# A graph layer on one core: the first adjacency unit multiplied piece by piece, its layer norm moved to GpSimd

## What is computed

```python
h = jnp.maximum(_layernorm(x, axis=-1), 0.0)          # x: 4096 x 128
# for each of two branches (features h, and features x2), adj: 4096 x 4096
ax = a @ x
h = ax + (1.0 + eps[0]) * ax
for i in range(3):
    h = jax.nn.relu(h @ W[i].T + b[i])
# then
merged = jnp.concatenate((out1, out2), axis=1)
x = x + merged @ Wm.T + bm
```

## Time and profile before

| | us |
|---|---|
| median of three runs | 408.82 |
| lowest and highest run | 408.42, 409.11 |
| the profiled execution, its whole time | 408.38 |
| its span, first to last instruction | 406.9 |
| PE busy | 402.3 (99%) |
| DVE busy, ACT busy | 219.5, 220.2 (54% each) |
| POOL busy | 30.2 (7%) |

### The profile page before, as it was taken

The page is one execution under the profiler, slowest core; times in us unless marked ns, Lnnn a source line. Parts: engine busy times, 40 slices in busy tenths (PEclk is TensorE's granted clock), DMA queues, the critical chain, the costliest instruction groups (busy, mean ns, idle before and its releaser), DMA issues.

```text
span 406.9 us, 4872 instructions
## 1 busy us (share of the span) xinstructions
PE 402.3 (99%) x1774; PEld 328.7 (81%) x1774; DVE 219.5 (54%) x260; ACT 220.2 (54%) x259; POOL 30.2 (7%) x35
## 2 busy tenths in 40 slices
PE   8999999999999999999999999999999999999996
PEld 3888888888888888888888888888888888888886
DVE  5888887655455334551645517445373444755223
ACT  5876667658474623555434556334565335766034
POOL 1223332100000000000100001000000000000100
PEclk9999999999999999999999999999999999999999
DMA  7998785744645174235584336653175550840100
GB/s 259 423 404 308 304 317 208 254 186 132 232 180 176 58 258 184 106 132 200 149 315 152 114 146 231 233 206 130 77 258 206 206 198 35 270 170 0 52 2 26
DMA packets 14317, 76.21 MB, mean 187 GB/s; under 512 B 1952, under 2 KB 2208, under 8 KB 6368
## 3 DMA queue, kind: packets, MB, share of 16 engines
q1 hardware_dynamic: 12960, 71.97, 47.4%
q0 software_dynamic: 1200, 3.93, 3.0%
q10 hardware_dynamic: 144, 0.13, 0.1%
HBM read 73.93 MB, written 2.10 MB: 187 GB/s over the span
## 4 chain that ended last, share of the span: by engine, by line
PE 99%; DVE 0%; issue 0%; DVEq 0%
PE acc L510 25%; PE acc L506 25%; PE acc L507 25%; PE second_acc L506 3%; PE second_acc L510 3%; PE second_acc L507 3%; PE hidden L507 3%; PE hidden L506 3%; PE hidden L510 3%; PE merged L514 2%; PE merged L507 1%; PE merged L506 1%; PE merged L510 1%; PE acc L534 0%; PE acc L549 0%; PE acc L544 0%
## 5 line engine op out<-in xcount | busy, mean ns | idle before, releaser
L506 PE MATMUL acc<-adj_hi,feat_lo 128*128 128x512 f32 x440 | 171.8, 390 | 0.0
L510 PE MATMUL acc<-adj_lo,feat_hi 128*128 128x512 f32 x440 | 171.7, 390 | 0.0
L507 PE MATMUL acc<-adj_hi,feat_hi 128*128 128x512 f32 x440 | 171.1, 389 | 0.0
L376 DVE TENSOR_TENSOR adj_lo<-adj_raw,adj_hi 128x2048 fp32r<-128x2048 f32 x48 | 108.3, 2288 | 37.9 <-ACT adj_hi L243 36.9
L243 ACT ACTIVATE adj_hi<-adj_raw 128x2048 fp32r<-128x2048 f32 x48 | 90.4, 1926 | 17.6 <-PE acc L510 15.8
L382 DVE TENSOR_TENSOR act_lo<-act_f,act_hi 128x512 fp32r<-128x512 f32 x60 | 41.0, 690 | 105.6 <-ACT act_f L263 105.6
L507 PEld LDWEIGHTS acc<-adj_hi,feat_hi 128*128 128x128 f32 x440 | 82.6, 188 | 17.7
L510 PEld LDWEIGHTS acc<-adj_lo,feat_hi 128*128 128x128 f32 x440 | 82.6, 188 | 17.8
L506 PEld LDWEIGHTS acc<-adj_hi,feat_lo 128*128 128x128 f32 x440 | 82.6, 188 | 17.3
L262 ACT ACTIVATE act_hi<-hidden,bias 128x512 fp32r<-128x512 f32 x45 | 31.0, 688 | 96.2 <-PE hidden L510 96.2
L438 DVE TENSOR_TENSOR adj_lo<-adj_raw,adj_hi 128x2048 fp32r<-128x2048 f32 x14 | 31.7, 2290 | 7.8 <-ACT adj_hi L284 7.8
(11 more groups left out here) (76 smaller groups left out, 238.0 us busy)
## 6 DMA issues: line engine op xcount, KB each, us to landing
adj_raw<-adj_tiles SPq DMA_DIRECT2D x62, 1024.0 KB, 5.1
x_rows<-x_tiles SPq DMA_DIRECT2D x16, 256.0 KB, 6.9
adj_raw<-adj_first SPq DMA_DIRECT2D x8, 256.0 KB, 5.1
x_res<-x_t POOLq DMA_DIRECT2D x8, 256.0 KB, 6.3
out_t<-y_sb POOLq DMA_DIRECT2D x7, 256.0 KB, 2.3
w_raw<-w_t SPq DMA_DIRECT2D x1, 512.0 KB, 5.8
out_t<-y_sb SPq DMA_DIRECT2D x1, 128.0 KB, 1.8
out_t<-y_sb ACTq DMA_DIRECT2D x1, 128.0 KB, 1.8
```

What stands on the lines that cost most here:

```text
L376: nc.vector.tensor_tensor(adj_lo[:, u % RING, :], adj_raw[:, u % RING, :], f32(adj_hi[:, u % RING, :]), ALU.subtract).then_inc(lo_made, 1)
L506: nc.tensor.matmul(out, lhs_lo, rhs_hi, start=start, stop=False)
L507: nc.tensor.matmul(out, lhs_hi, rhs_hi, start=False, stop=False)
L510: return nc.tensor.matmul(out, lhs_hi, rhs_lo, start=False, stop=stop)
```

## The change

- The order on PE is now step 0 for branch 1, step 0 for branch 0, then step 1 for both. Step 0 of branch 1 takes each piece as it comes: high by high, low features by high, and the high by low product of the piece before. The eight products of zeros between the first products are gone; the 15 ahead stay.
- The layer norm of unit 0 leaves ACT. POOL applies scale and shift in four operations of 128x128, in place in `x_rows`; ACT then makes the high part straight from that with a relu; POOL then makes the relu in place for itself (128x512) and subtracts. The other seven units keep their way.
- ACT makes that high part of branch 0 between the high parts of step 0 and those of step 1 (before, after both).
- Step 1 is loaded, and its high and low parts are made, in two halves of 128x1024 instead of four pieces.
- SP waits for the second piece of step 0 before it issues the loads of `x2`, `x` and adjacency of unit 1 and all that follow.

The diff, cut to its core:

```diff
             for s, (u, c) in enumerate(OPENING):
+                if s == len(PIECES):
+                    sp.wait_ge(fine_loaded[1], 16)
                 if c == 0:
                     load_x2(u)
                     load_x(u)
...
+            low_of_x2(0)
+            pool.wait_ge(x_loaded[0], 16)
+            pool.wait_ge(rstd_made, 1)
+            for j in range(JB):
+                last = nc.gpsimd.tensor_scalar(x_rows[:, 0, j, :], x_rows[:, 0, j, :], rstd[:, j:j + 1],
+                                               shift[:, j:j + 1], ALU.mult, ALU.add)
+            last.then_inc(first_norm_made, 1)
+            pool.wait_ge(feat1_hi_made, 1)
+            nc.gpsimd.tensor_scalar(x_rows[:, 0], x_rows[:, 0], 0.0, None, ALU.max).then_inc(first_relu_made, 1)
+            pool.wait_ge(first_relu_made, 1)
+            nc.gpsimd.tensor_tensor(feat_lo[:, 0, 0:JB, :], x_rows[:, 0], f32(feat_hi[:, 0, 0:JB, :]),
+                                    ALU.subtract).then_inc(feat1_lo_made, 1)
...
-            for u in range(U - 2):
+            high_of_x2(0)
+            std_of_x(0)
+            high_of_opening(0)
+            act.wait_ge(first_norm_made, 1)
+            nc.scalar.activation(feat_hi[:, 0, 0:JB, :], x_rows[:, 0], ACT.Relu).then_inc(feat1_hi_made, 1)
+            high_of_opening(1)
+            for u in range(1, U - 2):
...
+                if b == first:
+                    for i in parts:
...
+                        add(feat_hi, adj_hi, i)
+                        if i == 0:
+                            pe.wait_ge(feat2_lo_made, u + 1)
+                        add(feat_lo, adj_hi, i)
+                        if i > 0:
+                            low_ready(i - 1)
+                            add(feat_hi, adj_lo, i - 1)
+                    low_ready(parts[-1])
+                    add(feat_hi, adj_lo, parts[-1])
+                else:
+                    for i in parts:
+                        add(feat_hi, adj_hi, i)
+                    for i in parts:
+                        add(feat_hi, adj_lo, i)
+                    pe.wait_ge(feat1_lo_made, u + 1)
+                    for i in parts:
+                        last = add(feat_lo, adj_hi, i)
+                    signal(u, b, last)
...
+            for at in range(len(PIECES)):
+                for b in BRANCH_ORDER:
+                    pieces_aggregate(at, b)
```

More of the change, by code:

```diff
@@ L120, in gnn_layer_kernel @@
         raw_loaded = [sem(f"raw_loaded{s}") for s in range(RING)]
-        fine_loaded = [sem(f"fine_loaded{s}") for s in range(FINE_LOADS * FINE_SIGNALS)]
+        fine_loaded = [sem(f"fine_loaded{i}") for i in range(sum(len(p) - 1 for p in PIECES))]
         x_loaded = [sem(f"x_loaded{s}") for s in range(X_SLOTS)]
@@ L160, in f32, with piece @@
             return ap.bitcast(F32)
+        def piece(s, i):
+            at = sum(PIECES[s][:i])
+            return range(at, at + PIECES[s][i]), (None if i == len(PIECES[s]) - 1
+                                                  else sum(len(p) - 1 for p in PIECES[:s]) + i)
         def quarter(q):
@@ L193, in _ @@
                     load_x(u)
[L194 to L198, removed]
+                if s < len(PIECES):
+                    source = (adj_first, adj_second)[s]
+                    for i in range(len(PIECES[s])):
+                        js, n = piece(s, i)
+                        cols = slice(js.start * CW, js.stop * CW)
+                        done = raw_loaded[s] if n is None else fine_loaded[n]
+                        sp.dma_start(adj_raw[:, s, cols], source[i]).then_inc(done, 16)
                 else:
@@ L216, in _, with low_of_x2 @@
         def _(pool):
-            for u in range(U):
+            def low_of_x2(u):
                 rows = slice(u * JB, (u + 1) * JB)
@@ L510, in product @@
                 return nc.tensor.matmul(out, lhs_hi, rhs_lo, start=False, stop=stop)
-            def idle_products(n):
-                for _ in range(n):
-                    nc.tensor.matmul(merged[:, :], zeros[:, 0:P], zeros[:, :], start=True, stop=True)
             def columns(u, j):
@@ L521, in opening_bank, with pieces_aggregate @@
                 return (second_acc if c else acc)[b]
[L523 removed]
+            def pieces_aggregate(s, b):
                 u, c = OPENING[s]
                 out = opening_bank(c, b)
[L527 to L551 removed]
@@ new lines, in pieces_aggregate, with add, low_ready @@
+                parts = range(len(PIECES[s]))
+                def add(feat, adj, i):
+                    for j in piece(s, i)[0]:
+                        slot, cols = columns(s, j)
+                        last = nc.tensor.matmul(out[:, :], feat[:, b, u * JB + j, :], adj[:, slot, cols],
+                                                start=(u == 0 and j == 0 and feat is feat_hi and adj is adj_hi), stop=False)
+                    return last
+                def low_ready(i):
+                    n = piece(s, i)[1]
+                    if n is None:
+                        pe.wait_ge(lo_made, s + 1)
+                    else:
+                        pe.wait_ge(fine_lo_made, n + 1)
```

95 lines of the change are left out of this document (40 added, 55 removed).

## The result

The changed kernel takes 410.39 us (median of six runs, 410.37 to 410.85) where the kernel before, in the runs beside it, takes 408.62 (408.29 to 409.11). The ratio is 1.0048, 95% interval 1.0037 to 1.0059: slower, by 1.8 us, where the forecast was 3.25 slower and the range began at 410.0. The profiled execution took 410.85.

What follows compares the result with a forecast made beforehand. PE, busy 99% of the span, was taken as the bound; POOL and DVE taking turns would delay step 2's low part to 23.4 and its product by 3.25 us: 408.82 + 3.25 gives 412.0, range 410.0 to 413.2.

Steps and rivals of the forecast that it cites:

- PE piece by piece: Opening on PE: without the eight zero products, the 12 products of step 0, branch 1 end near 9.9 us.
- The best case: PE's gain in the opening, capped by step 2's low part: product at 19.5 for 20.25, at best 0.75 us won.
- POOL's norm: POOL's four operations alternate with DVE's low parts of step 0 from 7.65; the norm is made at 10.85 us.
- ACT's wait: ACT, done with step 0's copies near 8.85, stands idle some 2 us on POOL ahead of its relu.
- POOL's relu: Unit 0's relu on 128x512, taken as 0.8 us, 11.7 to 12.5; POOL's subtraction then precedes DVE's first half.
- From `var_eps` to the low part of step 2: Unit 1's `var_eps` ends at 19.0; 4.43 us later, at 23.4, step 2's low part ends (19.42 before).
- PE's own stalls: PE's waits for branch 0's low part (13.9) and second half (17.5); at step 2 by 20.8, under the other bound.
- Turn about: Port shared by POOL and DVE: whoever waits enters at the next instruction boundary; product 3.25 us later, chance 0.52.
- rival 1: Whoever holds the POOL/DVE port keeps it over instructions in a row: 2.25 or 2.45 us later, 411.1 to 411.3, chance 0.27.
- Faster after all: Rival 2: POOL and DVE don't hinder each other, step 2's landing bounds: 0.75 us won, 408.1, chance 0.1.
- The clock: Rival 3: without zero products and with idle gaps, PE's clock may fall back; 2.4 us more, 414.4, chance 0.06.
- Parts at nothing: Parts said to cost nothing: ACT's dropped operations, SP's hold of unit 1's loads (5.75 to about 6.95), loads behind `lo_made`.

Runs made afterwards that it cites:

- experiment 3: Kernel before with only step 0 of branch 1 piece by piece on PE, without the zero products between: 407.85 us, ratio 0.9990.
- 10: Three attempts: ACT's high part from scaled relu, DVE's float32 copy, no hold, step 2 off the square root; then ordering waits; then 12 zero products: 409.23, 408.96, 409.04 us.
- experiment 9: Changed kernel without POOL's relu of unit 0 in the low part of the features: 409.46 us, ratio 1.0028.
- Experiment 7: Changed kernel with step 2's parts made without waiting for the square root of unit 1: 410.59 us, ratio 1.0047.
- 8: Changed kernel with the norm back on ACT and step 2's parts not waiting for unit 1's square root: 407.91 us, ratio 0.9981.
- experiment 2: Changed kernel with PE's earlier order, both steps for branch 1, then both for branch 0: 411.37 us, ratio 1.0078.
- 4: Changed kernel without SP's wait ahead of the loads of unit 1: 410.53 us, ratio 1.0054.
- 1: Changed kernel with unit 0's norm back on ACT, still ahead of step 1's halves; POOL only subtracts: 409.01 us, ratio 1.0018.
- 5: Changed kernel with constants instead of rstd and shift in POOL's four norm operations: 409.77 us, ratio 1.0030.
- experiment 6: Changed kernel with DVE's low parts of step 0 waiting until POOL has made the norm: 411.03 us, ratio 1.0060.

## Why the prediction was right, and where it was off

The direction holds, and the time lies in the range, but with luck: 0.6 us of the loss lie outside the span, where the sum had nothing. Without them the time would be 409.8, under the range's 410.0. In the span the forecast was 3.25 (408.82 + 3.25 is 412.07, given as 412.0) and 1.3 to 1.6 came, half of it, and the chain named for it is not the one that ended last. By its steps:

- **PE piece by piece.** Predicted: 12 products by 9.9. They ended at 10.56: the first real product started at 7.34, not 6.79, and the rest is as said. The best case, 0.75 won, never came in any run; the product came earlier than before by 0.33 (experiment 3) and at most 0.6 (10). In 3 it was step 1's pieces that were late next.
- **POOL's norm.** Predicted 10.85, with operations 0.9 to 1.0 apart; made at 11.11. The end is right within 0.3, its way is not: I let each operation in after one subtraction of DVE and had DVE lose 0.9 for it. In the trace the first two take 1.53 and 1.39, and DVE loses 0.12 over its four (2.70 for 2.58). My 0.35 for one alone is 0.44. That end within 0.3 is two errors against each other.
- **ACT's wait.** Predicted some 2 us, measured 1.97.
- **POOL's relu, the step that failed.** I took 0.8 between the ends 0.10 and 1.26; it takes 1.49, outside both. (The 0.77 us of the Trainium skill's GPSIMD Engine Reference, which the prediction sets beside it, stands in the section "Elementwise — side-by-side cycle accounting"; the measured 1.49 is nearly twice that.) By my sum the subtraction asked before DVE's first half and that half waited for it, 13.85 to 15.05. It asked at 13.43, when that half was running (12.82 to 14.05): the half was not delayed, the subtraction was (1.74), then the second half (2.28), then `x2` (2.27). So on DVE its halves end at 16.25 for 17.5, `var_eps` at 17.65 for 19.0: the order in which the two met was wrong, not only a size. That a relu of 0.8 would have given the longer chain was not run, and experiment 9 speaks against taking it for granted: with no relu at all the subtraction did go ahead, and the halves ended earlier still.
- **From `var_eps` to the low part of step 2.** Predicted 4.43, measured 22.09 - 17.65 = 4.44. So on this chain the low part at 22.09 for 23.4 is the error of the step above and no other.
- **PE's own stalls.** I had branch 0's low part at 13.9 and PE at step 2 by 20.8, under the other bound. This failed too: the same relu and the delayed subtraction put it at 15.22, and PE at 21.70. The chain that ended last runs over these stalls and not over `var_eps`, which the prediction named. Experiment 7 shows what I missed: with `var_eps` taken off, 410.59.
- **Turn about or port kept.** Neither holds throughout. In the norm DVE ran on almost unhindered, as in the first half of rival 1: it had DVE's pieces over at 9.65, the norm at 11.05, the relu on ACT at 11.8, `var_eps` at 17.8 and the low part at 22.4; measured are 10.00, 11.11, 11.77, 17.65 and 22.09. Its rows are nearer than those of the turn about, which had 0.52. But its two halves in a row are not what happened: where whole subtractions meet (1.74, 2.28 and 2.27), they take turns. When they don't meet in that order, as in 9, two halves run in a row in 2.54. The Trainium skill, SBUF — State Buffer, section "Who interferes with whom", says that who issues first has the shared ports for the whole instruction and the other blocks; for whole subtractions these rows agree.
- **The other rivals.** Faster after all: no, in the changed kernel ACT did not wait for the transfer of step 2. It did so again only where step 2 was taken off `var_eps` (7, 8 and 10) and in 3. The clock: full in the changed kernel, but the rival is real; it came in experiment 2 after a wait of 2.30, by the mean clock in three of six executions.
- **Parts at nothing.** The hold is nothing (4), though one reason given for it misreads: the 2.8 us are those of a load of 256 KB, a quarter of the one that took 8.4. Nothing is given back after step 2: span less product is the same.
- **What the sum could not hold.** Some 0.6 us between the whole time and the span (2.09 for 1.50) came on top of 1.3 to 1.6 in the span. My 3.25 was for the span alone. In the other runs it was 1.51 (3), 1.81 (1), 1.74 (8), 1.86 (9), 1.6 (10), 2.1 to 2.2 (2, 4 to 7): it is large where POOL does the norm and its relu. No view shows what it is, and its cause stays open.

So: the norm on POOL costs 1.2 to 1.4 us (1). Leaving out its relu gives 0.9 back (9), constants for its scalars 0.6 (5), and these are not to be added, since the same chains are shortened. The piece-by-piece start gives 0.5 (3); and the square root in front of step 2 costs 1.1 once POOL is out of the way (8), nothing while it is in it (7).

## What to carry to other kernels

An idle GpSimd is no free engine for work in SBUF while VectorE subtracts one SBUF tile from another: its four operations took 3.78 us there and 1.74 alone, and whoever waits on them (here ScalarE, with five other things queued behind) hands the delay on. Look at what would run beside the moved work, not at the engine's busy share. When two chains end within 0.1 us of each other, shortening one shows nothing: experiments 6 and 7 are that case, one for each chain, while 1, 5 and 9 shorten both and win. And before a good combination is put down to its newest part, it has to be held against the plainest part alone: 8 wins no more than 3. Where an operation's duration has no row, write down also at which duration the order flips in which two engines meet; here the order was the error, though no run shows what the forecast duration would have given.

## What the runs showed of the hardware

- A `tensor_scalar` on GpSimd, float32 in SBUF, takes 0.44 us for 128x128 with VectorE still, and 1.49 for 128x512 with one input and VectorE idle for its first 0.96 us. That is more than a subtraction of two inputs of the same size alone (1.26 to 1.30). How much of the 1.49 is a wait for VectorE was not measured; beside VectorE's pieces of 128x512 it takes 1.93 (experiment 6).
- Beside VectorE's subtractions of about 0.7 us the 128x128 takes 0.59 to 0.73 with constants and 0.87 to 1.78 with its two scalars in SBUF (the first two operations in the changed kernel and in 2, 4 and 7).
- TensorE's clock fell to 1.2 GHz behind one idle time of 2.30 us, in the trace and, by the mean clock, in three of that kernel's six executions, and not behind two of 1.3 us, 2.1 us of work apart.
- When it first rises differs from trace to trace, though the 15 zero products are the same: their weight loads become denser than 0.43 between 4.8 and 5.3 us in experiments 1, 3, 8 and 9, near 6.05 before and in 5 and 6, near 6.6 in 2, near 6.9 in the changed kernel and in 4 and 7. Each kernel has one trace, so whether this goes with the kernel or with the execution is not shown. In 4 and 7 the first real product waits behind them: ACT's first copy was over at 6.57 and 6.66, the product ran at 7.09 and 7.13. In the changed kernel that copy was over only at 7.19, and the product ran at 7.34.
- A last store of 128 KB took 2.8 to 3.0 us instead of 1.8 in three kernels, as said in 10.
